# Eight stages of a decoder on one core: the engines' loops over the batches written out in line

## What is computed

```
x = LN(x + L0_attn(x))          # causal attention with rope, 16 heads of 8, then a gelu FFN
x = LN(x + L0_xattn(x, ctx))    # retention: 16 heads, decay mask, norm per head, gate
x = LN(x + L0_ffn(x))           # attention of 16 heads, then 8 experts (top 2) and a shared one
x = LN(x + L1_attn(x))          # Mamba in both directions: 256 channels, 16 states, conv of 4
x = LN(x + L1_xattn(x, ctx))    # attention with the softmax over the 8 heads
x = LN(x + L1_ffn(x))           # gated FFN; weights, inputs and products rounded to a grid
```

## Time and profile before

| stage | first to last instruction, us | length, us | granted TensorE clock |
|---|---|---|---|
| first attention | 16.0 to 346.9 | 331 | 0.99 |
| gelu FFN | 357.8 to 443.4 | 86 | 0.89 |
| retention | 451.9 to 765.3 | 313 | 0.77 |
| second attention | 773.7 to 1110.9 | 337 | 0.90 |
| experts | 1129.4 to 1581.5 | 452 | 0.95 |
| mamba | 1586.5 to 2612.8 | 1026 | 0.95 |
| cross attention | 2617.8 to 2879.6 | 262 | 0.66 |
| quant FFN | 2884.8 to 3131.2 | 246 | 0.66 |

### The profile page before, as it was taken

How to read it: one execution, slowest core, us unless ns; L and a number is a source line. 1 busy time by engine, 2 the same in 40 slices (tenths; PEclk the granted TensorE clock), 3 DMA queues, 4 the chain that set the end, 5 groups by cost and what they waited for, 6 DMA issues and landing times. The chain is left out here.

```text
span 3140.3 us, 56345 instructions
## 1 busy us (share of the span) xinstructions
PE 2281.8 (73%) x20075; PEld 1447.7 (46%) x20075; DVE 2202.8 (70%) x3826; ACT 1556.2 (50%) x2529; POOL 1422.3 (45%) x1127
## 2 busy tenths in 40 slices
PE   4888657774777769998958889988888975552703
PEld 3555445553555535565524445545544543341303
DVE  4887546885677735555528888787788884888698
ACT  4888425552777722222236656665665652221460
POOL 5555234555322200000008898888888983322001
PEclk9999877886899979999979999999999997665856
DMA  1000010000000010000022222222222220000000
GB/s 39 1 0 0 8 33 16 15 13 4 1 0 0 1 46 1 0 0 0 0 59 77 71 78 73 69 72 69 79 72 62 82 68 26 19 13 8 0 0 27
DMA packets 109830, 94.41 MB, mean 30 GB/s; under 512 B 12256, under 2 KB 106352, under 8 KB 109552
## 3 DMA queue, kind: packets, MB, share of 16 engines
q1 hardware_dynamic: 109680, 92.26, 10.2%
HBM read 83.32 MB, written 2.62 MB: 27 GB/s over the span
## 5 line engine op out<-in xcount | busy, mean ns | idle before, releaser
L1939 POOL TENSOR_TENSOR mam_h<-mam_h,mam_c_all 128x1024 f32<-128x1024 f32 x256 | 645.3, 2532 | 115.8 <-DVE mam_h L2011 115.3
L2011 DVE TENSOR_TENSOR_SCAN mam_h<-mam_decay,mam_ps_b 128x1024 f32<-128x1024 f32 x256 | 574.6, 2275 | 157.7 <-PE mam_ps_b L1642 151.8
L1642 PE MATMUL mam_ps_b<-mam_diag,mam_duT 64*128 64x128 f32 x4096 | 297.9, 290 | 117.5 <-DVE mam_h L2011 92.6
L1642 PEld LDWEIGHTS mam_ps_b<-mam_diag,mam_duT 64*128 64x128 f32 x4096 | 255.2, 193 | 273.5 <-issue 183.2
L1833 ACT ACTIVATE mam_decay<-mam_delta,mam_a_neg 128x508 f32<-128x508 f32 x512 | 330.3, 709 | 38.3 <-DVE mam_h L2011 38.1
L1661 PE MATMUL mam_ps_y<-mam_h,all_ident 64*64 64x512 f32 x2048 | 253.5, 609 | 10.0 <-POOL mam_h L1939 10.0
L519 DVE TENSOR_REDUCE at_top<-at_ps_s 128x4 f32<-128x512 f32 x256 | 174.6, 682 | 121.2 <-PE at_ps_s L359 121.2
L1234 ACT ACTIVATE moe_silu<-moe_ps_g 128x512 f32<-128x512 f32 x144 | 86.0, 597 | 291.7 <-PE moe_ps_g L1181 263.2
L437 ACT COPY at_probT<-at_ps_t 128x512 f32<-128x512 f32 x256 | 145.0, 589 | 116.9 <-PE at_ps_t L344 116.5
L198 POOL TENSOR_TENSOR at_parts_rest<-at_qk,at_parts 128x256 f32<-128x256 f32 x64 | 42.8, 668 | 316.8 <-ACT at_parts L193 316.8
L1184 PE MATMUL moe_ps_u<-moe_ynT,moe_w_up 128*128 128x512 f32 x288 | 159.5, 637 | 36.4 <-DVE moe_hidden L1317 36.4
(11 more groups left out here) (348 smaller groups left out, 4961.2 us busy)
## 6 DMA issues: line engine op xcount, KB each, us to landing
mam_c_all<-mam_c_rows SPq DMA_DIRECT2D x256, 256.0 KB, 3.4
all_x_all<-in_x SPq DMA_DIRECT2D x8, 256.0 KB, 4.7
ret_xg<-all_x_all SPq DMA_DIRECT2D x32, 64.0 KB, 1.8
ret_ctx<-in_ctx SPq DMA_DIRECT2D x32, 64.0 KB, 1.9
mam_xg<-all_x_all SPq DMA_DIRECT2D x8, 256.0 KB, 4.1
xat_xg<-all_x_all SPq DMA_DIRECT2D x8, 256.0 KB, 2.4
xat_ctx<-in_ctx SPq DMA_DIRECT2D x8, 256.0 KB, 2.9
out<-qua_res SPq DMA_DIRECT2D x8, 256.0 KB, 2.3
```

What stands on the lines that cost most here:

```text
L1642: last = nc.tensor.matmul(ps_b[:, slot, odd, :, at // 2, x:x + HT], duT[r, d, s % DT, at, :], diag[r, chunk % SLOTS, at, :, :], start=True ...
L1939: nc.gpsimd.tensor_tensor(flat(h[:, slot, :, :, :, :]), flat(h[:, slot, :, :, :, :]), flat(c_all[:, chunk, :, :, :, :]), ALU.mult).then_in ...
L2011: nc.vector.tensor_tensor_scan(row(h[:, s % H_SLOTS, :, :, :, :]), row(decay[:, s % SLOTS, :, :, :, :]), row(ps_b[:, s % 2, :, :, :, :]), ...
```

## The change

Every `Fori` becomes a Python `for`, 27 places in all, of which the one in `all_steps` and the one in gelu's `looped` serve several engines. The body is then issued once for each i with i a plain number: no loop's register, no back branch, waits on constants, addresses that are constants. Nothing else changes: the same instructions on the same engines in the same order, the same semaphores and counts, the same buffers. Its core (the others are of the same form):

```diff
@@ all_steps
-    with engine.Fori(1, NG - 1) as i:
+    for i in range(1, NG - 1):
         for b in range(G):
             step(i, b)
@@ attention, DVE (retention alike)
             peeled, per_loop = steps.n, p["dve_steps"]
-            with dve.Fori(1, NG - 1) as i:
+            for i in range(1, NG - 1):
                 steps = Steps(dve, dve_steps, i * per_loop + peeled - per_loop, per_loop)
                 for b in range(G):
                     step(steps, i, b)
@@ gelu_ffn
-            with engine.Fori(0, LOOPS - 1) as i:
+            for i in range(0, LOOPS - 1):
                 step(i, True)
@@ moe, PE (ACT, POOL, DVE alike)
             group(0, True, first=True)
-            with pe.Fori(1, NG - 1) as i:
+            for i in range(1, NG - 1):
                 group(i, True)
@@ mamba, SP
             group(0, True, first=True)
-            with sp.Fori(1, NG - 2) as i:
+            for i in range(1, NG - 2):
                 group(i, True)
@@ cross_attention, DVE (SP, PE, ACT, POOL alike)
-            with dve.Fori(1, NG) as i:
+            for i in range(1, NG):
                 steps = Steps(dve, dve_steps, i * per_loop + PAIR_STEPS - per_loop, per_loop)
@@ quant_ffn, DVE (SP, PE twice, ACT, POOL, DVE again alike)
-            with dve.Fori(0, NG // U) as i:
+            for i in range(0, NG // U):
                 loop = Steps(dve, dve_steps, i * U + base, U)
```

More of the change, by code:

```diff
@@ L750, in _ @@
             normed(Steps(dve, dve_steps), 0, first=True)
-            with dve.Fori(0, LOOPS - 1) as i:
+            for i in range(0, LOOPS - 1):
                 steps = Steps(dve, dve_steps, i * (2 * HALF) + HALF, 2 * HALF)
@@ L851, in _ @@
                 bring_next(1, b)
-            with sp.Fori(2, NG) as i:
+            for i in range(2, NG):
                 for b in range(G):
@@ L1244, in _ @@
             group(0, True, first=True)
-            with act.Fori(1, NG - 1) as i:
+            for i in range(1, NG - 1):
                 group(i, True)
@@ L1260, in _ @@
             before.root(nc, pool, c, 0)
-            with pool.Fori(0, NG - 1) as i:
+            for i in range(0, NG - 1):
                 group(i, True)
@@ L1948, in _ @@
             group(0, True, first=True)
-            with pool.Fori(1, NG - 1) as i:
+            for i in range(1, NG - 1):
                 group(i, True)
@@ L2213, in _ @@
             group(1, True, second=True)
-            with pe.Fori(2, NG - 1) as i:
+            for i in range(2, NG - 1):
                 group(i, True)
@@ L2281, in _ @@
             group(0, first=True)
-            with pool.Fori(1, NG) as i:
+            for i in range(1, NG):
                 group(i)
@@ L2445, in _ @@
             nc.scalar.copy(w_T[:], ps_f[:, 0, :, 0:F]).then_inc(wT_ready, 1)
-            with act.Fori(0, NG // U) as i:
+            for i in range(0, NG // U):
                 for u in range(U):
@@ L2476, in _ @@
                 nc.gpsimd.partition_all_reduce(amax[:, columns], amax_part[:, columns], 128, bass.bass_isa.ReduceOp.max).then_inc(amax_ready, 1)
-            with pool.Fori(0, NG // U) as i:
+            for i in range(0, NG // U):
                 for u in range(U):
@@ L2648, in _ @@
             put_out(Steps(dve, dve_steps, base + U, 18), 0, True, first=True)
-            with dve.Fori(1, NG // U - 1) as i:
+            for i in range(1, NG // U - 1):
                 loop = Steps(dve, dve_steps, i * 18 + base + U, 18)
```

9 lines of the change are left out of this document (5 added, 4 removed).

## The result

The changed kernel takes **3118.99 us** (median of 6 runs, 3112.64 to 3120.95) against 3152.36 (6 runs, 3150.87 to 3164.57): ratio 0.9883, 95% interval 0.9865 to 0.9901. It is faster by 1.2%, 33.4 us between the medians. The interval stands for 31 to 43 us, and between the means it is 36.9.

A forecast was written before the change was run, and what follows sets the result against it. Mamba's PE back edges, then register waits on DVE's path, were taken to bound the kernel. Terms 16.5 + 5.7 + 5 + 2.3 + 1.0 + 1.4 + 1.5 = 33.4 us, from 3153.2 to 3119.8 us; range 3101 to 3137.

The forecast's parts named there:

- Step 1: Mamba: PE's taken back edges delay passes two to six; without them 16.5 us less.
- Step 2: Mamba: DVE's waits on registers at the norm and softplus steps, about 0.95 us a pass; 5.7 us less.
- whoever starts earlier waits for PE: Rival, whole kernel: register work is hidden again, only mamba's edges count, 3136.7 us; chance 0.12.
- Step 3: Experts: idle time at pass starts and behind the router goes; 5 us less, bounds 2 and 6.
- Step 4: Cross attention: DVE's idle time at pass starts, 2.3 us less; gelu: 0.52 us twice, 1.0 us less.
- Step 5: Retention: residual's address worked out behind a wait in 24 batches; 1.4 us less, middle of 0 and 2.9.
- Step 6: Quant: address work before the 48 maxima, with the other passes' ends; 1.5 us less, between 0 and 6.2.
- Step 7: Both attentions: constants and no edges give the same pace, so 0 for 24 batches twice.
- the streaming of code: All stages: more code to bring in on the instruction queues, covered by the engines' own work; costed at nothing.
- The slower rival: DVE, ACT, POOL, and PE outside mamba: new code stalls engines, 3255 us; chance 0.04 of net loss, 0.05 of losing half.
- The clock rival: Second attention: shifted timing changes the granted clock's falls, at most 17 us either way; chance 0.07 of over half the difference.

The follow-up runs named there:

- experiment 8: The changed kernel with two unused TensorE matmuls added in each mamba group, ahead of its wait for VectorE: 3105.84 us, ratio 0.9849.
- experiment 7: The changed kernel with loops of retention and quant put back, VectorE's in one run: 3121.26 us, ratio 0.9905; ScalarE's in another: 3118.47 us, ratio 0.9890.
- experiment 9: The changed kernel with unneeded mask matmuls issued in the second attention: 3101.82 us, ratio 0.9826; with two unused matmuls per mamba group as well: 3091.44 us.

## Why the prediction was right, and where it wasn't

The forecast of 3119.8 us, put down as 3119, was met by 3118.99, and the sum of 33.4 us by 33.4. That it is so exact is luck: the measurement can't tell 31 from 43 us, and the terms below were wrong in both directions.

- **Step 1, mamba's back edges, -16.5.** Right in mechanism, a little small: 19.7 us done alone, 19.9 undone. Passes two to six fell from 614.80 to 596.14 us with TensorE's loop in line, 18.7. But three things stand behind that number, of which the step had one. The edges' own price in the kernel before is the 16.5 us forecast, or 18.1 with the late scan of the earlier trace rows. TensorE's waits on registers came off with them, 119.34 to 118.6 us a pass, 6 x 0.7 = 4.4 us, a term that the prediction put at nothing without saying why: it took pass one as the length without a loop, and pass one has these waits. And the granted clock fell ahead of the last scan in three of the six passes, which took some 4.7 us back. In the six passes together 18.1 + 4.4 - 4.7 = 17.8, and 17.9 us was measured (734.14 to 716.21). The price of an edge isn't the stall alone either: behind four of the five taken branches the granted clock fell, to 0.50 from 2008.5 to 2011.9 us in pass three of before and at the same place in the three behind it.
- **Step 2, mamba's waits on registers, -5.7.** This step failed. Its saving is real (17.64 us where it was 18.23, 0.95 a pass) and none of it reached the end of the six passes. It moved the end of DVE's work against PE's so that the granted clock fell near the end of every pass, and the pass lost what it had gained: 716.12 us with VectorE's loop and without. All six passes of the changed kernel have the fall in every profile of this code, against three of six with DVE's loop back. The prediction's reason, "nobody to wait for", holds between the two scans and not for the pass: at its end DVE waits for PE. I had put "whoever starts earlier waits for PE" as a rival, and the clock as another, and didn't join them. With the fall covered (experiment 8) the passes sum to 707.55, 8.6 less, so the time was there to be had. The 118 us a pass that the prediction wanted to see didn't come without it: 119.2 was measured.
- **Step 3, experts, -5.** The edges' idle times went as read, 0.62 to 0.03. From a pass's last multiply to the next pass's first it is 10.06 to 10.10 us before and 9.60 after at the five taken edges and 9.86 and 9.59 at the entry, with no difference at the exit: 2.7 us. The pair of profiles shows -2.7 as well, the undoing +3.5. Within my bounds of 2 and 6, but 1.5 to 2 too much: of the 0.59 us that I gave each edge 0.46 came through, and the stage varies by 4 us between profiles of the same code.
- **Step 4.** Cross attention -2.3: measured -2.1, undone +2.1. Gelu -1.0: nothing in the stage's length (85.6 both times), though the bracket is gone there too. The traces show why: DVE waits for PE's `gelu_ps_y` later in the pass, 4.91 and 5.20 us before and 5.49 and 5.82 after, so it is not the engine that the stage waits for, and what it saved became idle time.
- **Step 5, retention, -1.4.** Too small, -5.3 in the pair. DVE's part is 4.5 us (experiment 7): it sets the pace there, the end of the bounds that I had halved, and one batch of each pass bears 0.3 us, not the 0.12 that I gave all.
- **Step 6, quant, -1.5.** Wrong place. The 0.17 us in front of the maxima stays with constants, so it was never register work. Of the gain of 2.9 VectorE's loops have some 1.3 to 1.5, in the last part (L2649), where 0.26 and 0.18 us of idle time went in each of two passes. Rows of that loop stood in the trace and I hadn't read them. The other 1.5 us or so came in the first part by the other engines' loops; by which of them stays open.
- **Step 7 and the streaming of code, 0.** Confirmed as far as it can be seen: 9.31 us a batch against 9.30, 86 more blocks, no new idle time by "issue" behind a pass's start, and on DVE four waits of 0.2 us that way in the whole kernel. The slower rival has nothing for it here.
- **The clock rival** is most of the reason why the two profiled executions differ by 21.8 us and the medians by 33.4. The second attention got 9.1 us longer between the profiles; over all profiles it is 337.2 to 344.6 us with the old code and 340.0 to 350.1 with the new. Whether the change made falls there somewhat more frequent stays open: the ranges overlap. Its bound was too small: a granted clock of 0.90 is a fifth of the time at half speed, not a tenth, and covering the falls made the stage up to 20 us shorter (experiment 9), not at most 17.

With what was measured the sum reads: TensorE's loop in mamba 18.7 to 19.7, DVE's waits there 0, experts 2.7 to 3.5, cross attention 2.1, retention 4.5 to 5.3, quant 1.3 to 2.9, together 29 to 34 us. The forecast mixed a step that came to nothing (5.7 us) and small excesses in steps 3 and 4 (1.5 to 2.3 and 1.2) with steps 1 and 5, which were too small by 5 to 7 us together.

## What to carry to other kernels

A back edge costs TensorE 3.3 to 4.9 us when its loop's body is long (2121 instructions and more here) and 0.2 us when it is short (up to 1568), so unroll the long ones first; elsewhere constant waits bring 0.1 to 0.6 us each, where an engine waits for itself or starts a pass and is the one that the others wait for (in gelu it wasn't, and nothing came of 0.5 us twice). Before a saving on another engine is added to a sum, ask what TensorE does in the time that opens: where its clock falls the saving can be lost, and a few matmuls that nobody needs, put beside such a wait, brought nearly as much here (27.6 us in two stages) as the whole change. And profile the kernel before twice, since a stage that differs by 7 us between two profiles of the same code can't bear a term of 5 us.

## What the hardware showed that was not expected

- The stall of a taken branch doesn't grow with the body: 3.3 to 4.9 us at 2121 instructions, 3.87 at some 2450, 3.4 and 3.7 at some 4200.
- With a long body PE's queue brought about two blocks of code more for each taken branch than the same code in line did (113 against 103 over five).
- TensorE's waits and addresses on registers cost 0.7 us in each mamba group of 119 us (119.34 against 118.6), in small parts at six of VectorE's waits.
- The granted clock fell from 1.00 to 0.53 after 4 us in which TensorE was busy for 1.92 us, with one wait of 2.08 us. 1.88 us of matmuls in that wait kept it at 1.00.
- More work for the engine with the most busy time made a stage shorter: 260.34 us busy in 326.6 us, instead of 250.07 in 346.3 (340.0 at best without the addition), the granted clock 0.94 instead of 0.88.
